# One attention-plus-experts kernel: the last pair's values by halves, and which rows reach the first expert by one-hot products

## The reference

```python
x = x + xattn(layernorm(x), ctx, q_w, k_w, norm_w, gate_w, gate_b)
x = x + ffn(layernorm(x), combine_weights, top_idx, W1, b1, W2, b2)

def xattn(hidden, memory, ...):
    normed = rmsnorm(hidden, norm_w)
    v_pool = concat([normed, memory], axis=1)
    logits = (normed @ q_w.T) @ (v_pool @ k_w.T).T * scale   # causal over the own rows
    h_tilde = softmax(logits) @ v_pool
    alpha = sigmoid(hidden @ gate_w.T + gate_b)
    return (1.0 - alpha) * hidden + alpha * h_tilde

def ffn(hidden, combine_weights, top_idx, W1, b1, W2, b2):   # 8 experts, 512 rows each
    x = hidden.reshape(-1, d)
    gathered = x[top_idx.T]
    h = gelu(gathered @ W1 + b1)
    out_e = h @ W2 + b2
    out = zeros_like(x).at[tok].add(out_e * w)
```

## Time and profile before

| | |
|---|---|
| time, median of 3 runs | 274.86 us (274.32 to 274.9) |
| the profiled execution's own time | 275.01 us |
| its span | 273.2 us, so 1.8 us lie around it |
| granted TensorE clock, mean | 0.996 of full speed |
| PE busy | 263.7 us (97%) |
| PE weight loads | 225.8 us (83%) |
| DVE busy | 218.4 us (80%) |
| ACT busy | 188.2 us (69%) |
| POOL busy | 156.9 us (57%) |
| DMA moved | 42.44 MB, mean 155 GB/s |

### The profile page before, as it was taken

The page is one execution under the profiler, slowest core; times in us unless marked ns, Lnnn a source line. Parts: engine busy times, 40 slices in busy tenths (PEclk is TensorE's granted clock), DMA queues, the critical chain, the costliest instruction groups (busy, mean ns, idle before and its releaser), DMA issues.

```text
span 273.2 us, 5127 instructions
## 1 busy us (share of the span) xinstructions
PE 263.7 (97%) x1477; PEld 225.8 (83%) x1477; DVE 218.4 (80%) x553; ACT 188.2 (69%) x349; POOL 156.9 (57%) x152
## 2 busy tenths in 40 slices
PE   7899999999989999999999999999999999999993
PEld 3688899999876888888888888888888888888983
DVE  1899999899985779968878896796887889689453
ACT  2687899887666975786676587668657758773540
POOL 4349765565768717656456466655645656514525
PEclk9999999999999999999999999999999999999998
DMA  5986257588446945454464544645446561210211
GB/s 154 341 232 199 94 154 200 148 231 270 133 149 150 388 154 157 129 169 155 134 208 154 156 142 135 168 118 207 160 138 180 160 181 56 59 35 34 65 49 69
DMA packets 30560, 42.44 MB, mean 155 GB/s; under 512 B 5521, under 2 KB 24283, under 8 KB 30416
## 3 DMA queue, kind: packets, MB, share of 16 engines
q1 hardware_dynamic: 25120, 29.74, 35.0%
q0 software_dynamic: 4608, 12.24, 15.4%
q10 hardware_dynamic: 816, 0.26, 0.4%
HBM read 33.54 MB, written 9.24 MB: 157 GB/s over the span
## 4 chain that ended last, share of the span: by engine, by line
PE 81%; DVE 6%; issue 4%; DMA 4%; POOL 1%; ACT 1%; SPq 0%; DVEq 0%; POOLq 0%
PE bank L1423 19%; PE bank L1202 12%; PE bank L1203 12%; PE bank L1204 12%; PE bank L1424 10%; PE bank L1250 4%; PE bank L1294 3%; DMA x_all<-in_x_dram 2%; PE bank L1351 2%; DMA x_all<-token_rows,idx_all 2%; PE bank L1370 1%; PE bank L1371 1%; PE bank L1374 1%; PE bank L1318 1%; POOL out_dram L557 1%
## 5 line engine op out<-in xcount | busy, mean ns | idle before, releaser
L752 ACT ACTIVATE keysT<-bank,biasT 128x512 f32<-128x512 f32 x63 | 43.6, 692 | 55.6 <-PE bank L1204 39.3
L557 POOL DMA_INDIRECT out_dram<-h,sidx x32 | 36.7, 1146 | 40.2 <-DVE h L1094 34.8
L547 POOL DMA_INDIRECT x_all<-out_dram,idx_all x32 | 36.6, 1143 | 23.6 <-DMA out_dram<-h,sidx 16.0
L1202 PE MATMUL bank<-x_hi,w_parts 128*128 128x512 f32 (+1 forms) x114 | 45.1, 396 | 0.0
L1203 PE MATMUL bank<-x_lo,w_parts 128*128 128x512 f32 (+1 forms) x114 | 44.4, 389 | 0.0
L1204 PE MATMUL bank<-x_hi,w_parts 128*128 128x512 f32 (+1 forms) x114 | 44.1, 387 | 0.0
L1119 DVE TENSOR_TENSOR g_lo<-keysT,g_hi 128x512 fp32r<-128x512 f32 x32 | 22.1, 692 | 27.0 <-ACT g_hi L753 26.3
L543 POOL DMA_INDIRECT x_all<-token_rows,idx_all x28 | 30.7, 1095 | 18.9 <-DVE factor L1143 12.4
L1423 PE MATMUL bank<-w_parts,g_hi 128*128 128x512 f32 x112 | 40.5, 396 | 0.0
L1124 DVE TENSOR_TENSOR w_parts<-w_raw,w_parts 128x512 fp32r<-128x512 f32 x56 | 38.4, 686 | 0.0
L758 ACT CAST w_parts<-w_raw 128x512 fp32r<-128x512 f32 x56 | 34.9, 623 | 0.0
(11 more groups left out here) (187 smaller groups left out, 681.5 us busy)
## 6 DMA issues: line engine op xcount, KB each, us to landing
w_raw<-in_L_ffn_W_dram SPq DMA_DIRECT2D x32, 512.0 KB
idx_rows<-in_L_ffn_top_idx_dram SPq DMA_DIRECT2D x8, 256.0 KB, 4.1
out_dram<-x SPq DMA_DIRECT2D x8, 256.0 KB, 2.9
hn_cnat<-in_ctx_dram SPq DMA_DIRECT2D x7, 256.0 KB, 2.8
token_rows<-xn SPq DMA_DIRECT2D x7, 256.0 KB, 2.2
hn_cnat<-in_L_ffn_b_dram SPq DMA_DIRECT2D x1, 1024.0 KB
x_all<-in_x_dram SPq DMA_DIRECT2D x3, 256.0 KB, 6.8
x_all<-in_x_dram SPq DMA_DIRECT2D x1, 768.0 KB, 9.4
```

What stands on the lines that cost most here:

```text
L547: g.indirect_dma_start(accg[:, t, :], None, flat, list_of(e, t)).then_inc(acc_in[t], 16)
L557: g.indirect_dma_start(flat, idx(sidx[:, t:t + 1].bitcast(U32), 0), newrow[:, t, :], None, bounds_check=N - 1, oob_is_err=False).then_inc( ...
L752: a.activation(g32[:, f % NG, :], ps_up[f % 2][:, :], ACT.Gelu_apprx_tanh, bias=bias)
L1202: t_.matmul(dst, lhs_hi, rhs_hi, start=first, stop=False)
```

## The change

Four things are done.

1. `EARLY_PAIRS` becomes 6. Pair 5 is stored and gathered like the pairs before it; its one-hot matrices, its high and low parts (one ScalarE cast, one VectorE subtraction) and their eight matmuls go. As no late product now comes first in the banks, two products of zeros (`junk`) open them.
2. In the last pair the probabilities' transposes, their copies and the values are made for each sequence by itself; the first sequence's transposes stand inside the gate product. Each sequence has its own PSUM bank for them.
3. In pair 6 VectorE makes pair 5's statistics ahead of pair 6's gate, and `shift` ahead of `h`; GpSimd makes `rstd` of pair 5 ahead of `expert0_lo`; ScalarE makes the query and pair 5's `xn2` ahead of the `tanh`.
4. TensorE's order behind the last pair is new.

```diff
     NG = 4
-    EARLY_PAIRS = NPAIR - 3
+    EARLY_PAIRS = NPAIR - 2
...
         list0_f = idx_rows[:, (IDX_PARTS - 1) * C:IDX_PARTS * C].bitcast(F32)
-        late_hi = [M_hi[:, :, :], gateT_hi[:, :, :], hnT_hi[:, 0, :, :]]
-        late_lo = [M_lo[:, :, :], gateT_lo[:, :, :], hnT_lo[:, 0, :, :]]
+        late_hi = [gateT_hi[:, :, :], hnT_hi[:, 0, :, :]]
+        late_lo = [gateT_lo[:, :, :], hnT_lo[:, 0, :, :]]
...
         ps_pv = banks[7][:, :].rearrange("p (b t) -> p b t", b=2)
+        ps_pT_last = [banks[6][:, 0:H].rearrange("p (j s) -> p j s", j=2),
+                      banks[1][:, 0:H].rearrange("p (j s) -> p j s", j=2)]
...
                         sp.wait_ge(first_rows_in[t], 16)
-                    for late in (LAST - 2, LAST - 1):
-                        sp.wait_ge(xn_rdy, 2 * late + 2)
-                        sp.dma_start(rows_v[:, 2 * late:2 * late + 2, 0:H], xn2[:, late % 2, :, :])\
-                            .then_inc(xn_out[late % 2], 16)
+                    sp.wait_ge(xn_rdy, 2 * r + 2)
+                    sp.dma_start(rows_v[:, 2 * r:2 * r + 2, 0:H], xn2[:, r % 2, :, :]).then_inc(xn_out[r % 2], 16)
...
                 else:
-                    if not is_last(p):
+                    if not is_last(p) and not is_last_but_one(p):
...
                     rstd(p - 1, 1 - s)
+                    if is_last_but_one(p):
+                        expert0_lo(p - 1)
...
             def attention(p, s, use):
-                if is_last(p):
-                    act.wait_ge(xn_rdy, 2 * p - 2)
-                    act.wait_ge(q_mm, NPAIR)
-                    a.copy(late_hi[0], xn2[:, s, :, :]).then_inc(late_hi_rdy, 1)
...
                     hn_transposed(p + 2, s)
-                act.wait_ge(pT_mm, p + 1)
-                a.copy(probsT, ps_pT).then_inc(pT_ev, 1)
+                if is_last(p):
+                    for b in range(2):
+                        act.wait_ge(last_pT_mm, b + 1)
+                        a.copy(probsT[:, b, :, :], ps_pT_last[b]).then_inc(last_pT_ev, 1)
+                else:
+                    act.wait_ge(pT_mm, p + 1)
+                    a.copy(probsT, ps_pT).then_inc(pT_ev, 1)
...
                     context_transposed(p + 1, 1 - s)
+                if is_last_but_one(p):
+                    query(p + 1)
+                    normalised_x2(p - 1, 1 - s, use - 1)
...
                 a.activation(gate_t, gate_t, ACT.Tanh, scale=0.5).then_inc(tanh_rdy, 1)
-                if not is_last(p):
+                if not is_last(p) and not is_last_but_one(p):
...
                     hn_rows(p + 3, 1 - s)
-                if not is_first(p):
+                if not is_first(p) and not is_last_but_one(p):
...
                     act.wait_ge(xn_rdy, 2 * p)
-                    a.copy(late_hi[1], xn2[:, 1 - s, :, :]).then_inc(late_hi_rdy, 1)
+                    a.copy(late_hi[0], xn2[:, 1 - s, :, :]).then_inc(late_hi_rdy, 1)
...
                 if not is_first(p):
-                    if not is_last(p):
+                    if not isinstance(p, int):
...
                     residual(p - 1, 1 - s, last_use)
+                    if is_last_but_one(p):
+                        stats2(p - 1, 1 - s)
+                        aggr2(p - 1, 1 - s)
...
                     x_stats(10, NB, 4)
-                else:
+                elif not is_last_but_one(p):
...
                 else:
-                    aggr2(p - 1, 1 - s)
+                    if is_last_but_one(p):
+                        shift(p - 1, 1 - s)
+                    else:
+                        aggr2(p - 1, 1 - s)
...
                 v.reciprocal(rinv[:, :], rsum[:, :]).then_inc(ri_rdy, 1)
-                if is_last(p):
-                    dve.wait_ge(late_hi_rdy, 1)
-                    dve.wait_ge(xn_rdy, 2 * LAST - 2)
-                    v.tensor_tensor(late_lo[0], xn2[:, s, :, :], late_hi[0].bitcast(F32), ALU.subtract)\
-                        .then_inc(late_lo_rdy, 1)
...
                     dve.wait_ge(x_steps, steps[0])
-                elif not is_last(p):
+                elif not is_last(p) and not is_last_but_one(p):
...
+            def last_probs_transposed(b):
+                if b == 0:
+                    pe.wait_ge(pT_ev, NPAIR - 1)
+                pe.wait_ge(exp_rdy, 2 * LAST + b + 1)
+                for j in range(2):
+                    last = t_.transpose(ps_pT_last[b][:, j, :], probs[:, b, j * S:(j + 1) * S], ident[:, :])
+                last.then_inc(last_pT_mm, 1)
...
                                             gateT_hi[:, k, :], gateT_lo[:, k, :], k == 0, k == KH - 1)
+                    if is_last(p) and b == 0:
+                        last_probs_transposed(0)
...
                         .then_inc(setup_mm, 1)
-                pe.wait_ge(exp_rdy, 2 * p + 2)
-                for b in range(2):
-                    for j in range(2):
-                        last = t_.transpose(ps_pT[:, b, j, :], probs[:, b, j * S:(j + 1) * S], ident[:, :])
-                last.then_inc(pT_mm, 1)
+                if is_last(p):
+                    last_probs_transposed(1)
+                else:
+                    pe.wait_ge(exp_rdy, 2 * p + 2)
+                    for b in range(2):
+                        for j in range(2):
+                            last = t_.transpose(ps_pT[:, b, j, :], probs[:, b, j * S:(j + 1) * S], ident[:, :])
+                    last.then_inc(pT_mm, 1)
...
                     hn_transposes(2, 0)
-                if is_last(p):
-                    pe.wait_ge(log_rdy, 2 * NPAIR - 1)
-                    pe.wait_ge(late_hi_rdy, 1)
-                    for b in range(2):
-                        late_rows(0, b, late_hi, first=b == 0)
-                pe.wait_ge(pT_ev, p + 1)
+                if not is_last(p):
+                    pe.wait_ge(pT_ev, p + 1)
...
                 for b in range(2):
+                    if is_last(p):
+                        pe.wait_ge(last_pT_ev, b + 1)
...
-            def late_rows(n, b, part, first=False):
+            def late_rows(n, b, part):
...
                     t_.matmul(ps_xT[k][:, :], part[n][:, b, k * P:(k + 1) * P], onehot[:, 2 * n + b, :],
-                              start=first, stop=False)
+                              start=False, stop=False)
...
             each_pair(pe, attention)
-            early_rows(range(1))
+            pe.wait_ge(log_rdy, 2 * NPAIR - 1)
+            for k in range(KH):
+                t_.matmul(ps_xT[k][:, :], junk[:, 0:P], junk[:, :], start=True, stop=False)
+            early_rows(range(2))
+            pe.wait_ge(late_hi_rdy, 1)
+            for b in range(2):
+                late_rows(0, b, late_hi)
+            early_rows(range(2, 3))
+            pe.wait_ge(late_hi_rdy, 2)
+            late_rows(1, 0, late_hi)
+            early_rows(range(NT - 1, NT))
...
                 late_rows(0, b, late_lo)
-            early_rows(range(1, NT - 1))
-            pe.wait_ge(late_hi_rdy, 2)
-            for b in range(2):
-                late_rows(1, b, late_hi)
-            early_rows(range(NT - 1, NT))
-            pe.wait_ge(late_hi_rdy, 3)
-            late_rows(2, 0, late_hi)
-            pe.wait_ge(late_lo_rdy, 2)
-            for b in range(2):
-                late_rows(1, b, late_lo)
...
                 cols = slice(k * P, (k + 1) * P)
-                pe.wait_ge(late_hi_rdy, 4)
-                t_.matmul(ps_xT[k][:, :], late_hi[2][:, 1, cols], onehot[:, 5, :], start=False, stop=False)
+                pe.wait_ge(late_hi_rdy, 3)
+                t_.matmul(ps_xT[k][:, :], late_hi[1][:, 1, cols], onehot[:, 3, :], start=False, stop=False)
                 for b in range(2):
-                    pe.wait_ge(late_lo_rdy, 3 + b)
-                    last = t_.matmul(ps_xT[k][:, :], late_lo[2][:, b, cols], onehot[:, 4 + b, :],
+                    pe.wait_ge(late_lo_rdy, 2 + b)
+                    last = t_.matmul(ps_xT[k][:, :], late_lo[1][:, b, cols], onehot[:, 2 + b, :],
...
```

16 lines of the change are left out of this document (10 added, 6 removed).

## The result

| | before | after |
|---|---|---|
| median of 12 runs each, on the same chip | 274.90 us (274.12 to 275.29) | 277.26 us (275.79 to 278.77) |
| ratio, 95% interval | | 1.0088 [1.0066, 1.011] |
| profiled execution | 275.01 us, span 273.2 | 275.82 us, span 274.0 |
| expert 0's first product in it | 83.51 us | 84.35 us |

The change is slower, by 0.9%. The forecast was 274.6 and the upper end of the range 275.7. The twelve runs of the changed kernel lie in three groups of four: 275.79 to 276.02 at a mean granted clock of 0.996 to 1.00, 277.21 to 277.31 at 0.991 to 0.992, and 278.17 to 278.77 at 0.987. The profiled execution belongs to the first group, so its trace holds only the smaller part of the loss, about 1 us. Further down, one execution each of numbers 3 and 12 (296.36 and 379.31 us) is far slower than its neighbours and is left out of the ratios.

A forecast was written before the change was run, and what follows sets the result against it. TensorE's queue was taken to bind by a hair, VectorE and GpSimd close behind. Of VectorE's 0.60 us saving 0.21 comes through, other terms 0; -0.25 taken, 275.01 to 274.76 profiled, median 274.6, range 273.9 to 275.7.

The forecast's parts named there:

- The bounds: Ahead of expert 0, TensorE's queue decides by a hair, with VectorE and GpSimd close behind.
- Pair 5 leaves the one-hot way: Pair 5's work removed: TensorE 1.4 us less, VectorE 0.60 us less, ScalarE one cast less.
- rival 4: TensorE's clock falls after its idle time ahead of the gathered rows: +2 to +4.5 us, 277; chance 0.06.
- The new wait: First gather also waits for pair 5's stored rows, landing at 71.28 as `x_plus_h` ended before: cost 0, bounds 0 to +1.9.
- the prediction's own sign: Trace test: forecast wrong if the gather starts before 71.2 or after 71.8.
- rival 1: Pair 7's `h` on VectorE is held behind GpSimd's `expert0_lo`: between -0.25 and +0.1, say 274.8; chance 0.2.
- Pair 6's order: VectorE's saving in pair 6 ends at its wait for TensorE's logits, which start at 68.62 regardless: nothing gained.
- The halves: Last pair's first-sequence transposes inside the gate product: hidden, 0 us, since TensorE is ahead of VectorE either way.
- Rival 2: Pair 5's store lands late, delaying gathers 0.1 per 0.1 beyond 2.2 us: +0.35 at 2.8, +1.65 at 4.1; chance 0.15.
- rival 3: GpSimd less late, rows landing 0.3 to 0.4 us earlier or gather not tied: -0.6 to -0.85, 274.1; chance 0.14.

The follow-up runs named there:

- number 3: Changed kernel with pair 5's `expert0_lo` moved on GpSimd from behind pair 5's `rstd` to behind pair 7's `x_plus_h`; 276.41 us, ratio 1.0053.
- number 12: Changed kernel without the halves, with filler products on TensorE (4 ahead of the gathered rows, 6 behind); 276.15 us, ratio 1.0052.
- number 1: Changed kernel run again without any edit, for a profile of its slower runs; 278.32 us, ratio 1.010.
- number 6: Changed kernel without the halves: last pair's transposes, copies and values for both sequences together, behind the gate product; 278.14 us, ratio 1.0118.
- number 8: number 3 with pair 6's `rstd` behind two gathers instead of three, and filler products on TensorE (6 and 2); 275.29 us, ratio 1.0036.
- number 10: number 8 with GpSimd's fourth gather between the two last `rstd`, TensorE's tail in operand order, fillers only ahead of gathered rows; 274.68 us, ratio 1.0001.
- number 2: Changed kernel with filler products on TensorE in its two gaps, seven ahead of the first gathered rows, six behind; 275.95 us, ratio 1.0037.
- number 9: number 5 with filler products on TensorE, three between the first two gathered tiles and four behind them; 274.69 us, ratio 0.9998.
- number 7: Kernel before the change with only pair 6's new order added; 275.15 us, ratio 1.002.
- number 11: number 7 with `expert0_lo` on GpSimd moved behind pair 7's `x_plus_h`; 274.93 us, ratio 1.0006.
- number 4: Changed kernel with pair 5 back on the one-hot way, keeping the halves and pair 6's order; 275.68 us, ratio 1.0033.
- number 5: Changed kernel with gathers waiting only for pairs 0 to 4, pair 5's rows left out of expert 0; 276.05 us, ratio 1.0037.

## Why the prediction was wrong, point by point

**The bounds** were read rightly: GpSimd's three gathers and `rstd`, VectorE and TensorE's queue lay within half a microsecond of each other. In the change GpSimd decides, and VectorE, ScalarE and TensorE wait behind it in turn.

**Pair 5 leaves the one-hot way.** VectorE's 0.60 us did not come: 0.06 by the distance from the logits, 0.01 in number 1. The work is gone, but the time went into the wait for the gate product that the halves interrupt. Where that wait is away, most of it comes: 6.05 and 6.07 us to the last pair's first step without the halves (numbers 6 and 12), 5.97 where `shift` is not held (numbers 3, 8 and 10), against 6.49. In the change this costs nothing, as VectorE stands still for 1.29 us ahead of `shift` anyway, in the place named. TensorE's 1.4 us less work was counted as no gain, which was right; as idle time it was counted only in rival 4, and only for one gap, which was the second error (below).

**The new wait: the step that failed.** Its cost was put at 0, by a sum in which the rows land as `x_plus_h` ends. By the prediction's own sign, a gather after 71.8, this is where it failed: the gather came at 72.79. Of its terms, the store's 2.2 us was right (2.3, issued at 69.55 where 69.1 was forecast). Two were missing.
- `shift` of pair 5 was taken at its short duration. It was held for 1.06 us. The prediction saw the same trap for `var_eps` and for `h`, and gave it to rival 1, but the swap puts `expert0_lo` directly behind `rstd`, and the instruction that waits for `rstd` is `shift`, on the way to the store. The prediction had `xn2` wait for `rstd`, while the row that it cites names `shift`. That the stage as a whole ran 0.47 us earlier in this execution (logits at 68.15) hides part of it in the clock times. The Trainium skill, "SBUF — State Buffer", section "Who interferes with whom", has the port pair kept for a whole instruction by whichever engine is first; the row at 67.11 agrees, with a lead of 0.06 us.
- The gather was taken to start 0.18 us after its last condition, the row's "issue" of before. That is the lag of a gather behind work of its own queue. One that had waited for another engine stood in the trace of before, at 101 us:

```profile
100.94 0.17 DVE L1143 TENSOR_TENSOR factor<-total,x_all 128x4 f32<-128x4 f32 x1
```

```profile
101.92 1.39 POOL L543 DMA_INDIRECT x_all<-token_rows,idx_all  x1 [6.10 <-DVE factor L1143]
```

`factor` ended at 101.11, so that gather started 0.81 us later; in the five other places where this pair stands in that trace it is 0.80 or 0.81. With both terms the prediction's own sum is 69.1 + 1.06 + 2.2 + 0.86 = 73.22 for the gather, 1.8 us late, and the trace has 72.79 in a stage that ran 0.47 earlier. Numbers 2 and 9 price the wait: 1.28 us over the kernel before with fillers and wait, 0.10 with fillers and without the wait, so 1.2 us, and 16.18 against 14.84, so 1.3, from the logits to expert 0. Number 3 takes 0.94 of it for the held `shift`.

**Pair 6's order** was to cost nothing. In the kernel before it costs 0.2% (number 7), so the step was off by half a microsecond. With the hold removed that is not distinguishable from zero (number 11), but neither is number 11 distinguishable from number 7.

**The halves** were to cost nothing in the change, and cost nothing (number 12). But the reason given did not hold. The exponential was to be done when TensorE is at that place; TensorE waited 0.45 us for it, and VectorE 0.30 for the gate product, so TensorE was not "ahead of VectorE either way". Both waits were hidden by the late `rstd`, so the 0 was right in part by luck. In numbers 3, 8 and 10, where `shift` is not held, TensorE does not wait there; with pair 5's cast back it waits 1.35 us (number 4).

**Rival 2** (a late gather, slower) was the right direction: at its rate of 0.1 for 0.1 it gives +1.6 for an `rstd` that was 1.11 + 0.47 us late against its stage; from the logits of pair 7 to expert 0 it took 16.20 us instead of 14.89, so 1.31. It had named the store as the cause, the one term that held.

**Rival 4, the clock**, was given 0.06 and happened in eight of twelve runs. Its time of 277 was about right (277.3 and 278.5); of its +2 to +4.5 the slowest group has 2.6 over the first, the middle one only 1.4. The chance was wrong, because it was judged by the length of one gap, of which 1.02 us had done no harm. But the prediction had itself removed four products behind that gap and forecast a second wait on ScalarE right after it. Number 5 shows the clock falling in most runs with two gaps of 0.80 and 0.94 us and little between them. The Trainium skill, "TensorE: Matmul & The Clock Gate", section "What's actually happening", says that "the default state is throttled, and activity releases the throttle". Number 2 agrees: with work without any use the median is 275.95, against 278.32 for the change in number 1.

**Rivals 1 and 3.** `var_eps` did end with `normed` (66.29 and 66.27). `h` was not stretched (0.72 at 68.26); `shift` was, in its place. Nothing landed early.

## What to carry to other kernels

Taking work off an engine that waits anyway makes its idle time longer; for TensorE, add up the gaps and the work between them over the whole stretch before counting removed products as harmless, and price a fallen clock on everything behind. For a wait that moves from an engine's own queue to a semaphore, take the lag from a row of the same instruction that was released by another engine. When an instruction is swapped behind a producer, look at the producer's consumer on the other engine, here VectorE: it will be issued at just that moment. And before two traces are compared by the clock, count both from a common event ahead of the change: one kernel's executions lay half a microsecond apart here (68.15 and 68.64).
